# A two-layer gated graph network with residual norm: quads held on chip, split constants, and eps as a 65th column

## The reference, cut to what matters

```
def _ggc(x, adj, W, wih, whh, bih, bhh):
    m = adj @ (x @ W)
    gi = m @ wih.T + bih
    gh = x @ whh.T + bhh
    r, z = sigmoid(i_r + h_r), sigmoid(i_z + h_z)
    n = tanh(i_n + r * h_n)
    return (1.0 - z) * n + z * x

h = relu(_ggc(x, adj, W1, ...1)); h = relu(_ggc(h, adj, W2, ...2))
x = layernorm(x + h)                       # (x - mean) / sqrt(var + 1e-5)

mask = (adj != 0); rank = cumsum(mask, axis=1); deg = rank[:, -1:]
k = minimum(deg, 100); pos = rank - (deg - k)
w = mask * where(pos > 0, 0.5 ** (k - pos), 0.0)
x = layernorm(x + w @ (x @ weight) + bias)
```

## Time and profile before

| | us |
|---|---|
| median of 3 runs (351.58 to 351.70) | 351.69 |
| the profiled execution | 351.6 |
| its span, first to last instruction | 349.8 |
| PE busy | 329.6 (94%) |
| DVE busy | 303.6 (87%) |
| ACT busy | 184.3 (53%) |
| granted TensorE clock, mean | 0.996 |
| DMA, 16 engines: mean rate, moved | 318 GB/s, 111.10 MB |

### The profile page before, as it was taken

The page is one execution under the profiler, slowest core; times in us unless marked ns, Lnnn a source line. Parts: engine busy times, 40 slices in busy tenths (PEclk is TensorE's granted clock), DMA queues, the critical chain, the costliest instruction groups (busy, mean ns, idle before and its releaser), DMA issues. The chain is left out here.

```text
span 349.8 us, 6790 instructions
## 1 busy us (share of the span) xinstructions
PE 329.6 (94%) x2536; PEld 154.2 (44%) x2536; DVE 303.6 (87%) x520; ACT 184.3 (53%) x240; POOL 24.0 (7%) x32
## 2 busy tenths in 40 slices
PE   1997999999999999999999989999999999999992
PEld 0441333233333333333333323544444444889992
DVE  0689879898999999998998669889899999878996
ACT  0202403114032165277377428878796969459993
POOL 2000000000000000000000001101020202022044
PEclk9999999999999999999999999999999999999998
DMA  6999999999999999999899999999999997000002
GB/s 244 414 409 409 409 407 409 409 409 404 402 374 333 389 369 335 358 378 326 303 336 334 382 411 406 341 341 347 355 407 353 388 369 296 17 3 4 2 33 90
DMA packets 32720, 111.10 MB, mean 318 GB/s; under 512 B 3632, under 2 KB 6192, under 8 KB 32688
## 3 DMA queue, kind: packets, MB, share of 16 engines
q1 hardware_dynamic: 31824, 109.20, 82.3%
q10 hardware_dynamic: 864, 1.48, 1.2%
HBM read 109.62 MB, written 1.05 MB: 316 GB/s over the span
## 5 line engine op out<-in xcount | busy, mean ns | idle before, releaser
L448 PE MATMUL m_acc<-stream,s_in 128*64 128x512 f32 x512 | 126.6, 604 | 3.6 <-DMA stream<-in_adj_t 2.8
L911 DVE TENSOR_SCALAR codes<-stream 128x1024 uint8<-128x1024 f32 x114 | 75.4, 687 | 6.2 <-DMA stream<-in_adj_t 5.9
L448 PE MATMUL out<-stream,s_mid 128*64 128x512 f32 x272 | 68.3, 593 | 0.1
L448 PEld LDWEIGHTS m_acc<-stream,s_in 128*64 128x64 f32 x512 | 34.4, 138 | 70.3 <-issue 48.1
L448 PE MATMUL m_acc<-stream,s_mid 128*64 128x512 f32 x240 | 54.8, 598 | 0.0
L960 DVE SCALAR_TENSOR_TENSOR codes<-codes,run 128x384 uint32<-128x384 uint32 (+2 forms) x62 | 43.9, 709 | 2.1
L955 DVE TENSOR_TENSOR run<-run,codes 128x768 uint16<-128x768 uint16 (+2 forms) x61 | 42.4, 696 | 2.4 <-DVE codes L960 0.5
L851 POOL TENSOR_TENSOR rstd<-var,mhalf 128x4 f32<-128x4 f32 x16 | 22.1, 1385 | 322.1 <-DVE var L1066 322.1
L678 ACT ACTIVATE rz<-gate_ps,b_rz 128x256 f32<-128x256 f32 x32 | 13.4, 468 | 45.4 <-PE gate_ps L516 45.3
L448 PEld LDWEIGHTS out<-stream,s_mid 128*64 128x64 f32 x272 | 19.5, 137 | 37.9 <-issue 37.3
L646 ACT ACTIVATE m_high<-m_acc 64x512 f32<-64x512 f32 x13 | 7.7, 593 | 52.6 <-PE m_acc L448 44.8
(11 more groups left out here) (139 smaller groups left out, 362.3 us busy)
## 6 DMA issues: line engine op xcount, KB each, us to landing
stream<-in_adj_t SPq DMA_DIRECT2D x204, 512.0 KB, 6.3
...
const<-in_consts ACTq DMA_DIRECT2D x1, 358.0 KB, 6.7
...
```

What stands on the lines that cost most here:

```text
L448: last = nc.tensor.matmul(to[D * u:D * (u + 1), :], state[:, t * D:(t + 1) * D], stream[:, n % SLOTS, u * CW:(u + 1) * CW], start=start[u] ...
L911: nc.vector.tensor_scalar(edges(p // 2, b, 2 * (p % 2), 2), stream[:, n % SLOTS, :], 0.0, None, ALU.not_equal).then_inc(mask_made, 1)
```

## The change

Loads and products:

- Six pairs are loaded into tiles of their own in place of a ring slot (`HELD`): pairs 0 and 1 of chunk 0, pairs 2 and 3 of chunk 1, pairs 12 and 13 of chunk 7. They lie in `wexp[:, 1]`, `late` (which also holds `x1s` and `sup_0`), `third` (`x_res`, `h_c`, bias, late constants) and `run[1]`.
- Pairs 0 and 1 of chunk 0 are multiplied for layer 2 in chunk 1, after its pairs 7 and 9, and pairs 2 and 3 of chunk 1 in chunk 2, after its pairs 8 and 11 (`product_held`). So `DONE` is `(1, 2, 2, 3, 4, 5, 5, 6)` where `TRI` is `(0, 1, 2, 3, 4, 5, 5, 6)`. Chunk 0 is now among the `KEPT` (one more copy, add and identity matmul). Pairs 12 and 13 of chunk 7 are multiplied in the turn, without a second load.
- The list of loads has 198 entries where it had 204; `ALONG_PAIRS` is 8, 10, 11, 11, 10, 10 where it was 8, 10, 12, 12, 11, 11.

Order: in chunks 1 and 2 the gates and what follows them stand earlier in the queues (1, 1, 2, 3, 3, 4, 5, 6). `combine(NCH)` on DVE stands after 4 steps of the chain, not 6. ACT makes one block more in step 6 of pass 2 and one less at the end; DVE in step 7 makes its first block ahead of `sum_squares`, not behind.

Constants: `consts` is 128x332 where it was 128x716; the weights of layer 2 come in a second array of 128x192 at the end of chunk 3, into `third`; the doubled `w_2` is built by a memset and two copies on ACT.

Eps: `sq` and `ysq` have 65 columns, the last filled once with eps, so that the sum of squares contains it; `add_eps` and `var` are gone.

```
-M2_BANK = {1: 1, 2: 2, 3: 1, 4: 2, 5: 3, 6: 1, 7: 2}
+M2_BANK = {0: 3, 1: 1, 2: 2, 3: 3, 4: 2, 5: 3, 6: 1, 7: 2}
-KEPT = range(1, 5)
+KEPT = range(0, 5)
+HELD = {0: (0, 1), 1: (2, 3), NCH - 1: (12, 13)}
+HELD_STEP = {1: (7, 9), 2: (8, 11)}
...
-TURN = [(0, 12), (0, 13), (1, 10), (1, 11), (1, 12), (1, 13), (2, 10), (0, 14), (0, 15),
+TURN = [(1, 10), (1, 11), (1, 12), (1, 13), (2, 10), (0, 12), (0, 13), (0, 14), (0, 15),
         (1, 14), (1, 15), (2, 11)]
...
-GATES, SIG, TT, TANH, NEWH, RELU, NODE, TO_MID = 2, 2, 4, 5, 5, 6, 8, 9
+GATES, SIG, TT, TANH, NEWH, RELU, NODE, TO_MID = [
+    (None, first, first) + (then,) * (NCH - 3)
+    for first, then in ((1, 2), (1, 2), (2, 4), (3, 5), (3, 5), (4, 6), (5, 8), (6, 9))]
...
-               6: (1, 2, 1), 7: (0, 1, 1), 8: (0, 2, 4)}
+               6: (1, 2, 2), 7: (0, 1, 1), 8: (0, 2, 4)}
 DVE_EXPANDS = {1: (0, 0, 0), 2: (0, 0, 0), 3: (0, 0, 0), 4: (0, 0, 1), 5: (0, 0, 1), 6: (0, 0, 3),
-               7: (0, 1, 1), 8: (1, 1, 5)}
-ACT_END = (2, 1, 1, 1, 1, 0, 0, 0)
+               7: (1, 0, 1), 8: (1, 1, 5)}
+ACT_END = (1, 1, 1, 1, 1, 0, 0, 0)
...
+                if n in HELD_AT:
+                    at = HELD_AT.index(n)
+                    if HELD_TURN[at]:
+                        sp.wait_ge(held_used, 1)
+                    sp.dma_start(held[HELD_IN[at]], adj_t[g, q]).then_inc(held_in[HELD_IN[at]], 16)
+                    return
-                if n >= SLOTS:
+                if n >= SLOTS and n - SLOTS not in HELD_AT:
                     sp.wait_ge(pair_used, n - SLOTS + 1)
...
+            def product_held(b, q):
+                first, last = b == 0 and q == HELD[b][0], q == HELD[b][-1]
+                pe.wait_ge(s_mid_made, b + 1)
+                done = pair(LOAD_AT[b, q], q, s_mid, m2_bank(b), [first] * 2, last)
+                if last:
+                    done.then_inc(held_used, 1)
...
                     product1(b, PAIRS[b][q])
+                    if b in HELD_STEP and q in HELD_STEP[b]:
+                        product_held(b - 1, HELD[b - 1][HELD_STEP[b].index(q)])
...
             def to_rstd(n, r):
-                pool.wait_ge(var_made, n + 1)
-                nc.gpsimd.tensor_tensor(rstd[:, r, :], var[:, r, :], mhalf[:, :], ALU.pow)
+                pool.wait_ge(sums_of_sq, n + 1)
+                nc.gpsimd.tensor_tensor(rstd[:, r, :], stat[:, r, :], mhalf[:, :], ALU.pow)
...
-            for j, k in CHAIN[0]:
+            for j, k in CHAIN[0][:4]:
                 chain(j, k)
             combine(NCH)
+            for j, k in CHAIN[0][4:]:
+                chain(j, k)
...
                 sum_squares(t - 1, 0, sq[:, :, :])
-                add_eps(t - 1, 0)
```

228 lines of the change are left out of this document (140 added, 88 removed).

## The result

The changed kernel takes 348.25 us (median of 4 runs, 347.68 to 349.01), against 351.69 for the kernel before in the same comparison: a ratio of 0.9904, 95% interval 0.9884 to 0.9924, so faster by 1.0%. The prediction was 348.2. The profiled execution took 348.46 (span 346.7) against 351.6, 3.14 less. The total came out as forecast, but its terms did not: their errors have both signs and cancel. In a second comparison the same two kernels took 347.95 and 351.98, a ratio of 0.9878 (0.9854 to 0.9901), so the gain was 3.44 the first time and 4.03 the second.

A forecast was written before the change was run, and what follows sets the result against it. Loads lead from 29.7 to 66.7 us, then PE in most of the rest, with a latency chain from 298.2 to 314.5. +0.2 - 1.35 - 1.4 - 0.55 - 0.4 = -3.5 on 351.6, median 348.2; 8-in-10 range 346.9 to 350.6.

The forecast's parts named there:

- Step A: Load-led stage to 66.67 us: four products added there are mostly hidden, net +0.2 us, bounds -0.5 and +3.4.
- Pass 1 after that: Rest of pass 1: same products on PE, so its 126.5 us move as a block, with no term of its own.
- Step B: Seam into pass 2: earlier gates sum gains 1.15 us, step 1's `make_x1s` without `add_eps` 0.19; -1.35 in all.
- Step C: Steps 2 to 6 of pass 2: PE loses 2.86 us, but node(7) needs DVE's h_c; -1.4, bounds -0.8 and -2.9.
- PE sets the pace: Rival: PE sets pass 2's pace to the end, so steps 2 to 6 give -2.9; 346.7 us, chance 0.10.
- Step D: Step 7's chain: power of about 1.05 us without DVE beside it, sigmoids 1.95 earlier, 0.55 more than the node; -0.55.
- Step E: End, from the node at 314.5 us: -0.23 for PE's wait for ACT, -0.2 for the last power; -0.4 in all.
- The other part: Very end: the power of the last chunks no longer waits behind `add_eps`, -0.2 us.
- the slower one: Rival: `n_input` stalls DVE's masks in chunks 1 and 2, so DMA loses time; 5.2 for +0.2, 353.1 us, chance 0.09.
- less than forecast: Rival: seam gives only 0.2 or held products cost 1 us more, and the power stays long; 350.2 us, chance 0.14.

The follow-up runs named there:

- e2: The changed kernel with three of the four held products in chunks 1 and 2 only 64 columns wide instead of 512; 347.2 us.
- e4: The changed kernel with a further transfer of 384 columns of zeros behind the small `consts`; 348.35 us.
- e5: The changed kernel run and traced once more, unchanged; 347.95 us.
- e6: The changed kernel with DVE's block of step 7 put back behind its sum of squares; 347.96 us.
- e7: The changed kernel without the identity products that add chunk 0's held sums in pass 2; 347.75 us.
- e9: The changed kernel with, in chunk 3, the sum for the gates one mask later and `n_input` and what follows one pair later; 347.46 us.
- e11: The changed kernel with a small add of zero on DVE behind every sum of squares, shaped like `add_eps`; 350.5 us.
- e12: The changed kernel with quad 1 of chunk 1 put back: its two pairs loaded again and multiplied in pass 2, not chunk 2; 348.29 us.

## Why the prediction was right, step by step

The range and the direction were earned by the mechanism; that the total came within 0.1 was luck. The sum holds because the errors of its terms cancel: +0.43, +0.71, -0.63, -0.43, -0.02, +0.34, together +0.40, against a forecast of -3.5 and a measured -3.10 between the profiled executions. The trace of the kernel before, against which the sum was made, is one of its fastest executions, and the trace after is one of the changed kernel's slower ones.

- **Step A, mis-sized: +0.63 for +0.2.** The mechanism was right: the products fell among the waits for loads, and most of their 3.44 was hidden. In the seven traces the pair of 66.67 starts 0.36 to 0.71 later than in the one trace of the kernel before, so +0.2 was too little against each of them. The term at fault is the lateness of PE, laid out as 0.6 to 0.7: three narrow products take 0.79 to 1.14 away (e2). The 0.47 of the smaller `consts` is in the measured figure, since e4 without it is 0.42 to 0.77 later at this pair.
- **Pass 1 after that: "moves as a block" failed.** +0.71 in the first trace, and between -0.15 and +1.47 over seven from gates(2) to gates(7), against a single trace of the kernel before. The sign of it stood in the earlier trace rows already: DMA at a share of 0.98 and PE at 126.50 of 126.50 in the same window. With both full there is little to make up a delay with, and a PE that comes later frees the ring's slots later; that this carries the delay is argued and not shown. The traces with late waits for loads (after, e5, e6, e7) are also those with the longest stretch here. What starts those waits stays open: e2, with most of the held products gone, does not have a shorter stretch than others, and e9 only suggests an answer.
- **Step B, mis-sized: -1.98 for -1.35.** The seam gave 1.73 and not 1.15, since the 1.19 of the earlier trace rows was read as the gap. Counted in pairs of 0.86 from the same row the gap was 1.72. (The Trainium skill, "Perfetto Trace Analysis", "Summary: the profiler window per engine type", says that a matmul's end in a profile is an estimate; the 1.19 against 1.73 here is what that is worth.) `make_x1s` gave 0.25 where 0.2 was taken (e11: 0.21).
- **Step C, right in kind, mis-sized: -1.83 for -1.4, and by another path.** DVE's chain and not PE's work sets the pace: e7 takes 0.58 from PE and gains nothing, e11 gives DVE small adds and loses 0.63 up to gates(14) and 0.81 up to node(7). The rival "PE sets the pace" is out. But it is not at `h_c` of step 7 that PE meets the chain. From gates(14) to node(7) it takes 6.13 here and also in e12, where `h_c` was ready 1.07 before the node, so the 0.07 here is a near miss and no wait. PE meets the chain in step 6, at a block that ACT makes behind `tanh`, and `tanh` waits for DVE's `t_n`:

```profile
285.38 0.51 ACT L750 ACTIVATE n_g<-t_n,const 128x256 f32<-128x256 f32 x1 [2.24 <-DVE t_n L1070]
...
287.40 2.00 ACT L806 ACTIVATE wexp<-codes,code_bias 128x2048 uint16<-128x2048 uint8 x1
288.28 1.07 PE L626 MATMUL out<-codes,wexp 128*128 128x128 f16 x16
```

  PE's next block starts at 289.55, 0.15 after ACT's has ended. In the kernel before, ACT's block of step 6 was:

```profile
289.01 2.00 ACT L741 ACTIVATE wexp<-codes,code_bias 128x2048 uint16<-128x2048 uint8 x1
```

  Counted from gates(9) it ended at 74.23, and ends at 73.26 now: 0.97 earlier. From there to gates(14) it takes 7.19 and 6.33, 0.86 less, which is the one pair that left step 6. Together that is the 1.83. The 0.97 is also what `h_c` of step 6 gained: 0.62 for three adds, by e11, and 0.35 where a hole of DVE's in the kernel before went:

```profile
282.47 1.23 DVE L955 TENSOR_TENSOR run<-run,codes 128x2048 uint16<-128x2048 uint16 x1 [0.46 <-DVE codes L960]
```

  Of the 2.86 that PE was spared, the other 1.03 came back mostly as its waits for ACT: by the starts of the blocks 0.65 more than before in step 4 and 0.22 more in step 6. So the prediction was right that PE would wait at blocks that ACT has not made. The waits at the nodes of steps 4 and 6 did not come: PE reached them 0.05 and 0.38 after `h_c` was made. ACT idles 2.24 before its `tanh` in step 6, with that block behind it; whether the block can go ahead of `tanh` was not tried.
- **Step D, right: -0.57 for -0.55.** The power took 1.01, and the sigmoids came 6.07 after the node, where 6.25 was laid out. e6 gives 0.36 for the order; the rest was not split. The Trainium skill, "SBUF — State Buffer", "SBUF: two separate sides", has VectorE and GpSimd share a port pair under a lock that goes to whichever starts first. The trace of e6 agrees in that moving one DVE block turns 1.01 into 1.92. The end does not fit the "first": there a power recorded as starting 0.23 before a DVE block still ends 0.04 after two of them:

```profile
326.86 2.62 POOL L925 TENSOR_TENSOR rstd<-stat,mhalf 128x4 f32<-128x4 f32 x1 [7.33 <-DVE stat L1145]
327.09 2.35 DVE L1179 TENSOR_SCALAR codes<-codes 128x2048 uint16<-128x2048 uint8 x2
```

- **Step E, half failed: -0.06 for -0.4 in this trace, about -0.25 in the others.** The wait of 0.23 for ACT's last block is still there as 0.21, though ACT makes one block fewer. ACT was not what was late; it now waits for DVE's `y` in the same places:

```profile
327.21 0.42 ACT L887 ACTIVATE stream<-stream 128x256 f32<-128x256 f32 x1 [0.73 <-DVE stream L1243]
...
330.60 0.42 ACT L887 ACTIVATE stream<-stream 128x256 f32<-128x256 f32 x1 [1.08 <-DVE stream L1243]
```

  The other part came on the engines: from the start of the last blocks to DVE's last instruction it is 5.41 now, 5.66 before, 0.25 less for the 0.2 forecast. Behind it the output's transfer took 0.22 longer in this trace (2.47 after DVE's end, 2.24 before). From the last blocks to the end of the span it is 8.33 before, 8.30 here, but 8.08 to 8.17 in the ten other traces that leave the end alone, so the 0.2 is there as a rule. It came although the powers of the end got longer: all eight took 1.0 to 1.1 before, and five of eight take 1.48 to 2.62 now, each with a block of DVE's that starts right behind it, as in the rows under step D.
- Of the rivals, the slower one named DVE behind `n_input` in chunks 1 and 2. There it starts without a wait (33.85 and 56.40). DVE waits for ACT in chunk 3, 0.63 and 0.73 where it was only 0.29 before, and nothing near the rival's 5.2 came. The 350.2 of "less than forecast" is a slip: its three terms on 348.2 give 350.4.
